# The smallest neighbour pieces of both hidden parts in one PSUM bank, and new task orders on all engines

## The reference

```python
mask = (adj > 0.0).astype(x.dtype)
W1a, W1b = (W1[:F], W1[F:])
xj_proj = x @ W1a
diff = x[:, :, None, :] - x[:, None, :, :]
h = jax.nn.relu(xj_proj[:, :, None, :] + diff @ W1b + b1)
hm = jnp.einsum('bjkh,bjk->bjh', h, mask)
deg = jnp.sum(mask, axis=-1)
return hm @ W2 + deg[..., None] * b2
# and outside of it:
x = _layernorm(x + _L0_gnn_ref(x, adj, W1, b1, W2, b2), axis=-1)
```

## Time and profile before

| what | value |
|---|---|
| time, median of 3 runs | 254.54 us (254.0 to 255.02) |
| profiled execution, first to last instruction | 253.0 us |
| around it, to the median | 1.5 us |
| PE busy | 239.2 us (95%) |
| DVE busy | 230.0 us (91%) |
| ACT busy | 214.8 us (85%) |
| POOL busy | 133.1 us (53%) |

### The profile page before, as it was taken

One profiled execution on the slowest core, in us unless ns is written; L12 is line 12 of the kernel. 1 busy time (PEld: TensorE's weight loads), 2 busy tenths in 40 slices (PEclk: granted clock), 3 DMA queues, 4 the chain that ended last, 5 costly groups with the idle time before them and its releaser, 6 DMA issues. The chain is left out here.

```text
span 253.0 us, 9425 instructions
## 1 busy us (share of the span) xinstructions
PE 239.2 (95%) x2813; PEld 190.5 (75%) x2813; DVE 230.0 (91%) x810; ACT 214.8 (85%) x636; POOL 133.1 (53%) x288
## 2 busy tenths in 40 slices
PE   7968999999999999999999999999999999999990
PEld 2536687878887978878877878878887879777870
DVE  4797799999999999999999999999999999979853
ACT  2396999898989999898989989898989898988820
POOL 1415252565555574655554564655655555454834
PEclk9997999999999999999999999999999999999997
DMA  6992003501312203031212203031310110000001
GB/s 196 349 352 87 1 3 127 146 4 43 106 45 51 98 22 106 26 106 41 105 41 76 69 20 99 27 105 44 104 45 25 41 29 17 4 21 3 25 21 51
DMA packets 10552, 18.21 MB, mean 72 GB/s; under 512 B 1296, under 2 KB 7696, under 8 KB 10512
## 3 DMA queue, kind: packets, MB, share of 16 engines
q1 hardware_dynamic: 10512, 17.73, 21.7%
HBM read 15.63 MB, written 2.10 MB: 70 GB/s over the span
## 5 line engine op out<-in xcount | busy, mean ns | idle before, releaser
L1287 PE MATMUL ring<-hot,vh 128*128 128x128 bf16 (+9 forms) x768 | 115.8, 254 | 0.9 <-ACT ring L869 0.4
L1287 PE MATMUL ring<-hot,vl 128*128 128x128 bf16 (+9 forms) x768 | 113.9, 251 | 0.0
L1737 DVE SCALAR_TENSOR_TENSOR sums<-ring,sums 128x256 f32<-128x256 f32 (+14 forms) x304 | 104.9, 375 | 8.7 <-PE ring L1287 4.0
L1287 PEld LDWEIGHTS ring<-hot,vh 128*128 128x128 f16 (+1 forms) x768 | 61.0, 102 | 18.9 <-issue 7.9
L874 ACT COPY ring<-u_sb 128x144 f32<-128x144 f32 (+13 forms) x256 | 65.2, 302 | 9.6 <-DVE sums L1737 7.9
L1287 PEld LDWEIGHTS ring<-hot,vl 128*128 128x128 f16 (+1 forms) x768 | 62.2, 103 | 2.8
L631 POOL TENSOR_TENSOR vl<-vf,vh 128x384 f16<-128x384 f32 x32 | 34.4, 1075 | 49.2 <-ACT vf L839 32.3
L869 ACT COPY ring<-u_sb 128x512 f32<-128x512 f32 (+1 forms) x80 | 45.0, 565 | 0.9 <-PE ring L1111 0.4
L1710 DVE TENSOR_SCALAR hot<-slotT 128x944 bf16<-128x944 f16 (+6 forms) x112 | 28.5, 267 | 0.0
L685 POOL TENSOR_TENSOR sums<-taken,sums 128x512 f32<-128x512 f32 x16 | 20.3, 1272 | 11.7 <-ACT taken L891 11.7
L790 ACT CAST maskT<-bx 128x512 bf16<-128x512 f32 x32 | 18.4, 583 | 8.8 <-PE bx L1139 7.7
(11 more groups left out here) (117 smaller groups left out, 470.8 us busy)
## 6 DMA issues: line engine op xcount, KB each, us to landing
adj_sb<-adj SPq DMA_DIRECT2D x16, 512.0 KB, 3.5
x_sb<-x_pairs SPq DMA_DIRECT2D x16, 128.0 KB, 2.3
xT_sb<-xT SPq DMA_DIRECT2D x16, 128.0 KB, 2.4
x_all<-x SPq DMA_DIRECT2D x4, 512.0 KB, 8.1
out<-o_sb SPq DMA_DIRECT2D x16, 128.0 KB, 1.7
wts<-weights SPq DMA_DIRECT2D x1, 417.0 KB, 4.8
cst_general<-general SPq DMA_DIRECT2D x1, 256.0 KB, 2.7
cst_half<-half SPq DMA_DIRECT2D x1, 137.0 KB, 3.2
```

The lines of the kernel that those rows point to most:

```text
L1287: return eng.matmul(to if part == "main" else to[g * HT:g * HT + HT], values, selection, start=False, stop=final, skip_group_check=True)
L1737: eng.scalar_tensor_tensor(out=to, in0=view(pair, part, unit, piece), scalar=0.0, in1=to, op0=ALU.max, op1=ALU.add).then_inc(added[part], 1)
```

## The change

Three things are changed.

1. The last unit now holds pieces 8, 9 and 10 of the main and the tail part together, in one main bank (`JOINT`): one seed function (`seed_joint`) with three copies over all six groups, one clamp, and two adds (`add_joint`) instead of four. PE still gathers main and tail by separate matmuls. Piece 7 moves to the unit of piece 4 (main) and of pieces 4 to 6 (tail).
2. `project`, `unsort_y` and `gather` can be cut into steps, and the steps of `project` and `unsort_y` are put between those of `gather`.
3. The task orders of DVE, ACT, PE and POOL are new, in the prologue, the body and the epilogue.

```diff
-UNITS = {"tail": [[0, 1], [2, 3], [4, 5, 6], [7, 8, 9, 10]], "main": [[0], [1], [2], [3], [4], [5, 6], [7, 8, 9, 10]]}
+UNITS = {"tail": [[0, 1], [2, 3], [4, 7, 5, 6], [8, 9, 10]], "main": [[0], [1], [2], [3], [4, 7], [5, 6], [8, 9, 10]]}
...
+JOINT = {part: NU[part] - 1 for part in PART}
+RING_UNITS = {"tail": NU["tail"] - 1, "main": NU["main"]}
...
+            def seed_joint(pair):
+
+                eng.wait_ge(u_copied["main"], pair.n + 1)
+                eng.wait_ge(u_copied["tail"], pair.n + 1)
+                released(pair, "main", JOINT["main"] - BUFFERS)
+                for piece in UNITS["main"][JOINT["main"]]:
+                    _, _, cap, slots = PIECES[piece]
+                    v = u_sb[pair.side][:, :, 0:cap]
+                    last = eng.copy(joint_view(pair, piece),
+                                    v if slots == 1 else v.unsqueeze(3).broadcast_to([P, GROUPS, cap, slots]))
+                last.then_inc(seeded["main"], 1)
...
+            def add_joint(pair, piece):
+
+                nth = JOINT_ADDS.index(piece)
+                if nth:
+                    eng.wait_ge(joint_added, len(JOINT_ADDS) * pair.n + nth)
+                else:
+                    for part in PART:
+                        eng.wait_ge(gathered[part], NU[part] * (pair.n + 1))
+                        eng.wait_ge(added[part], ADDS[part] * (pair.n + 1))
+                    eng.wait_ge(clamped, pair.n + 1)
+                to = sums[pair.side][:, :, 0:PIECES[piece][2]]
+                eng.scalar_tensor_tensor(out=to, in0=joint_view(pair, piece), scalar=0.0, in1=to,
+                                         op0=ALU.max, op1=ALU.add).then_inc(joint_added, 1)
...
             masks(Pair(0, 0))
             count_masks(Pair(0, 0))
...
+            masks(Pair(0, 2))
+            count_masks(Pair(0, 1))
+            count_least(Pair(0, 1))
             select(Pair(0, 0), 0)
             select(Pair(0, 0), 1)
...
             run(eng, body)
-            gather(Pair(0, 14), "main", 6)
+            keep_busy_last(7)
             gather(Pair(0, 15), "main", 0)
```

More of the change, by code:

```diff
@@ L1273, in gather @@
-            def gather(pair, part, unit):
-                if unit == 0:
-                    eng.wait_ge(vl_ready, 2 * (pair.n + 1))
-                pieces = UNITS[part][unit]
-                eng.wait_ge(hot_ready, NPIECES * pair.n + pieces[-1] + 1)
-                eng.wait_ge(seeded[part], NU[part] * pair.n + unit + 1)
+                    else:
+                        last = eng.matmul(to, sums[pair.side][:, t, :], w2ts[scaled(pair)][:, :, :].rearrange("p g o -> p (g o)"),
+                                          start=False, stop=True, skip_group_check=True)
@@ new lines, in project, with unsort_y @@
+                if end == 3 * NT:
+                    last.then_inc(y_ready, 1)
+            def unsort_y(pair, first=0, end=TILES):
+                if first == 0:
+                    eng.wait_ge(y_copied, pair.n + 1)
+                    eng.wait_ge(permT_copied, pair.n + 1)
+                for c in range(first, end):
+                    g, t = divmod(c, NT)
+                    last = eng.matmul(bx3[:, (TILES + c) * O:(TILES + c + 1) * O], permT[pair.side][:, c, :],
+                                      y_sb[:, t * 2 + g, :], start=True, stop=True)
+                if end == TILES:
+                    last.then_inc(z_ready, 1)
@@ new lines, in gather @@
+            def gather(pair, part, unit, first=0, end=TILES):
+                pieces = UNITS[part][unit]
+                if first == 0:
+                    if unit == 0:
+                        eng.wait_ge(vl_ready, 2 * (pair.n + 1))
+                    eng.wait_ge(hot_ready, NPIECES * pair.n + max(pieces) + 1)
+                    if unit == JOINT[part]:
+                        eng.wait_ge(seeded["main"], NU["main"] * (pair.n + 1))
+                    else:
+                        eng.wait_ge(seeded[part], RING_UNITS[part] * pair.n + unit + 1)
@@ L1372, in body @@
                 if has(1):
-                    gather(new, "main", 5)
+                    gather(new, "tail", 2)
+                    gather(new, "main", 5, 0, 1)
                 if has(3):
@@ L1805, in body @@
                 if has(0):
+                    select(pair, 0)
+                    select(pair, 1)
+                if has(1):
+                    count_least(new)
+                if has(0):
                     select(pair, 2)
                     select(pair, 3)
+                if has(-1):
+                    add(old, "main", 1)
+                    add(old, "tail", 2)
                 if has(1):
```

671 lines of the change are left out of this document (345 added, 326 removed).

## The result

The changed kernel takes **274.86 us** (median of 4 runs, 274.57 to 274.98); the kernel before took 254.44 beside it. The ratio is 1.081, interval 1.079 to 1.083. The prediction was 256.1, with a range up to 258.9: slower, as forecast, but by 20 us instead of 2. Times are medians of all runs of a kernel; the ratios further down leave out one slow run each of aligned_start and residual_early, whose medians without it are 263.18 and 256.24.

A forecast was written before the change was run, and what follows sets the result against it. Three engines were read as close to full, PE with 13.56 us of own work in a 14.01 us period. Span 253.0 + 4.5 (start) - 2.9 (periods) + 0 (end) = 254.6, median 256.1; range over all 252.6 to 258.9.

The forecast's parts named there:

- The period, "13.80 us": Loop body: time a pair falls from 14.01 to 13.80 us, bounds 13.5 and 14.1.
- The gain of order and bank, -0.21 us a pair: Loop body: PE's old waits and load time removed, new waits added; -2.9 us over 14 periods.
- The joint bank, "by itself it is worth nothing": DVE and ACT lose instructions beside PE's work: no gain until PE's waits are gone, bounds 0 and 0.3 us a pair.
- The start, +4.5: Prologue: two DVE tasks wait for DMAs, delaying pair 1's permutation; +4.5 us, bounds +1.5 and +5.5.
- The end, 0: Epilogue: dummy matmuls move ahead of pair 15's gathers, last pair's chain slightly longer; 0 us, bounds -1 and +1.
- The waits in the new order, "0.12": Loop body: PE loses 0.12 us a pair waiting for z and 0.12 for `perm`.
- The rivals: Four alternatives: shorter period 0.15, start absorbs late DMA 0.12, new waits eat the gain 0.15, time unchanged 0.08.
- the sign: Whole kernel: slower than before, chance 0.50; within 0.5% 0.30; faster 0.20.
- Rival 3: Loop body: new waits by `count_given` or `add_small` eat the order's gain; period 14.05, whole 259.6 us; chance 0.15.

The follow-up runs named there:

- aligned_start: Changed kernel with VectorE and GpSimd instructions reordered against collisions, VectorE's permutation ahead of main adds 4 and 7, and the start's two waits put back: 263.60 us.
- residual_early: aligned_start with GpSimd's residual ahead of its sum of the taken piece instead of behind both low halves of v: 256.27 us.
- short_pool: Changed kernel with GpSimd's six long instructions cut to 4 columns a tile from the third pair on, the rest left uncomputed: 254.71 us.
- start_moved: Changed kernel with the start alone put back: maximum of x behind the first permutation, pair 2's mask behind pair 0's last slot: 270.36 us.

## Why the prediction was wrong

- **The period, "13.80 us": wrong, and this is the step that failed.** I took every duration on VectorE over from the rows of before and reckoned only with waits and with work removed. 15.17 was measured, 13.71 where GpSimd's long instructions are cut short. VectorE's busy time makes the difference: 14.87 - 13.35 = 1.52 us a pair, 21 us in 14 periods. GpSimd's new order entered the sum only as a link behind `count_given`; that it starts `vl`, the sum of the taken piece and the scaling just ahead of `perm`, the own slots and `rest` was not priced. A row of before would have told it: `vl` at 116.61 with 1.35 us, beside a median of 0.92, while `perm` of the earlier trace rows ran.
- **The gain of order and bank, -0.21 us a pair: there where GpSimd is out of the way, and a little too small.** With the same cut in both kernels the changed one has 0.28 us a pair less (13.71 against 13.99), 3.9 us in 14 periods, where I had 2.9. How order and bank share it was not measured.
- **The joint bank, "by itself it is worth nothing", bounds 0 and 0.3: wrong on the side of cost, in the order of before.** I priced the instructions it removes and not what it ties together: it carries piece 7 over to unit 4, whose release the joint seed needs. In that order the bank costs 6.4 us, and 18.6 with one add misplaced. In the new order short_pool shows no such loss, and in the changed kernel ScalarE stands at the joint seed for 12.4 us in all, but TensorE waits for it only once, 0.6 us.
- **The start, +4.5: right in size, its reason in part.** x landed 0.6 us earlier than worked out, the adjacency at 17.63 for 17.35, `perm` of pair 1 at 23.68 for 22.8, and the whole +4.3. Its size is in the profile of short_pool too (37.73). But with both waits put back only 2.4 us of it went; the other 1.9 I had no term for, so the close agreement is partly luck. What the start is worth at the end is less sure, as the run start_moved shows.
- **The end, 0: right within its bounds,** -0.6.
- **The waits in the new order, "0.12" each for z and `perm`:** TensorE's first waits in the changed kernel are

```profile
PE bx L1171 <- DVE perm L1661: 5.8, 13, 1.3
PE bx L1225 <- DVE z L1843: 5.7, 12, 0.7
```

some 0.4 us a pair each, and the list leaves out short gaps (it has none for z in the kernel before, where I had read 0.22 a pair). By the starts, as I had counted, it is more. In the changed kernel's pair shown above, the matmuls ahead were through at 172.40 and 174.56:

```profile
173.08 0.39 PE L1225 MATMUL bx<-perm,excess 128*128 128x128 bf16 x4 [0.52 <-DVE z L1843]
...
175.19 0.39 PE L1171 MATMUL bx<-perm,mask 128*128 128x128 bf16 x4 [0.47 <-DVE perm L1661]
```

0.68 and 0.63 lost. In a pair of short_pool they were through at 173.91 and 175.44:

```profile
173.96 0.39 PE L1231 MATMUL bx<-perm,excess 128*128 128x128 bf16 x4
...
175.52 0.39 PE L1177 MATMUL bx<-perm,mask 128*128 128x128 bf16 x4
```

0.05 and 0.08. So these two terms were sound without collisions, and the collisions made them more than five times what I had. (The sum for `perm` gives 2.75 + 0.25 - 2.85 = 0.15, not 0.12.)
- **The rivals and the sign.** None of the four named a longer instruction. Rival 3 had the right sign and 259.6. That the forecast had the right sign too is mostly luck: it said slower because of the start, and the start is 4.3 of the 20 us, while 16.3 come from the periods, which I had at -2.9.

## What to carry to other kernels

When an order is changed on GpSimd and VectorE together, lay the two timelines side by side. For every VectorE instruction with two SBUF inputs, or comparing a tensor in SBUF with a scalar into SBUF, ask which GpSimd instruction will have started just before it: the price is about what is left of that one. Put GpSimd's long instructions beside reductions, statistics and adds from PSUM; where they must meet, let VectorE start first if it sets the pace. A duration in a profile is not a constant of the instruction: compare the minimum, median and maximum of its group before it is carried into a sum, and when two buffers are merged, look at which release the merged one now waits for.

## What the runs showed of the hardware

- Behind a GpSimd sum on 128x512 f32, started some 0.4 us before, the five forms of VectorE instruction with two SBUF inputs, or with one SBUF input and a scalar, grow by 738 to 750 ns each, from 132 to 870 as well as from 661 to 1411. GpSimd's time does not change. The add with one input from PSUM, the count and the statistics change by 0 to 2 ns. Started first, VectorE is undisturbed, and GpSimd's sum grows from 1.26 to 1.55 us beside `perm` and the mask.
- Such a stop is in no list of waits. It is in the length of the instruction, as busy time.
- Collisions wander. Three moves took 1.1 us a pair off the instructions that were hit, and 0.9 came back on others, most of which had not been hit before.
